# One PSUM bank moved from VectorE's ring to ScalarE's ring in a four-layer transformer kernel

## The reference

```python
x = x + attn_a(layernorm(x))      # rope attention: q, k, v and the output are rotated
x = x + ffn(layernorm(x))         # attention with biases, then a mixture of 8 experts, top 2
x = x + attn_b(layernorm(x))      # scores = cov(q, k) / d + q_var * k_var / d
x = x + ffn(layernorm(x))         # the same ffn weights again
# each attention: softmax(q k^T) v with 16 heads; ffn: gelu(t @ w1[e] + b1[e]) @ w2[e] + b2[e]
```

## Time and profile before

| | us |
|---|---|
| median of 3 runs | 1138.43 (1137.03 to 1139.28) |
| the profiled execution, its own time | 1136.1 |
| its span in the trace | 1134.2 |
| TensorE busy | 1029.3 (91%) |
| VectorE busy | 558.4 (49%) |
| ScalarE busy | 602.7 (53%) |
| GpSimd busy | 383.0 (34%) |

### The profile page before, as it was taken

How to read it: one execution, slowest core, us unless ns; L and a number is a source line. 1 busy time by engine, 2 the same in 40 slices (tenths; PEclk the granted TensorE clock), 3 DMA queues, 4 the chain that set the end, 5 groups by cost and what they waited for, 6 DMA issues and landing times. The chain is left out here.

```text
span 1134.2 us, 22104 instructions
## 1 busy us (share of the span) xinstructions
PE 1029.3 (91%) x8516; PEld 774.6 (68%) x8516; DVE 558.4 (49%) x1358; ACT 602.7 (53%) x1118; POOL 383.0 (34%) x823
## 2 busy tenths in 40 slices
PE   2798898889998799999995899999999789999998
PEld 2565565556654699989994656556665479998997
DVE  3638777657873411121113687878778341111111
ACT  1336565657786344344431667768877544434342
POOL 5546676547852100000003534555784210000000
PEclk9669788879999799999995799999999879999999
DMA  8000000000000000000000000000000000000000
GB/s 262 2 2 1 2 3 2 3 2 3 3 3 3 1 1 1 1 1 1 1 1 1 2 2 3 2 3 3 2 4 2 2 1 1 2 1 19 1 10 10
DMA packets 9958, 10.41 MB, mean 9 GB/s; under 512 B 1528, under 2 KB 7552, under 8 KB 9856
## 3 DMA queue, kind: packets, MB, share of 16 engines
q1 hardware_dynamic: 8848, 7.64, 2.1%
q10 hardware_dynamic: 1008, 1.38, 0.4%
HBM read 7.44 MB, written 1.05 MB: 7 GB/s over the span
## 5 line engine op out<-in xcount | busy, mean ns | idle before, releaser
L873 DVE TENSOR_REDUCE M<-bankR 128x2 f32<-128x512 f32 x512 | 326.7, 685 | 140.6 <-PE bankR L357 139.6
L670 ACT ACTIVATE Pr<-bankE 128x512 f32<-128x512 f32 x512 | 277.1, 595 | 125.5 <-PE bankE L344 121.7
L764 ACT ACTIVATE KQ<-bankE,b1c 128x512 f32<-128x512 f32 x256 | 173.4, 689 | 219.0 <-PE bankE L596 217.1
L605 PEld LDWEIGHTS bankR<-w,KQ 128*128 128x128 f32 x2048 | 237.3, 192 | 4.9
L605 PE MATMUL bankR<-w,KQ 128*128 128x128 f32 x2048 | 237.7, 275 | 0.0
L1015 DVE SCALAR_TENSOR_TENSOR X<-bankR,WE,X 128x128 f32<-128x128 f32 x256 | 72.1, 344 | 324.7 <-PE bankR L605 324.7
L357 PE MATMUL bankR<-KQ 32*128 32x256 f32 x1024 | 175.3, 346 | 8.3 <-DVE M L873 4.8
L371 PE MATMUL bankO<-Pr,Vx 128*32 128x256 f32 x2048 | 170.7, 408 | 0.6 <-ACT OT L664 0.3
L344 PEld LDWEIGHTS bankE<-KQ 32*128 32x128 f32 x1024 | 79.9, 190 | 98.3 <-issue 65.8
L344 PE MATMUL bankE<-KQ 32*128 32x256 f32 x1024 | 133.3, 337 | 0.8 <-DVE b1c L920 0.8
L357 PEld LDWEIGHTS bankR<-KQ 32*128 32x128 f32 x1024 | 112.9, 196 | 21.1 <-DVE M L873 14.9
(11 more groups left out here) (175 smaller groups left out, 1187.8 us busy)
## 6 DMA issues: line engine op xcount, KB each, us to landing
THL<-in_w SPq DMA_DIRECT2D x1, 2048.0 KB, 10.0
KQ<-MT SPq DMA_DIRECT2D x128, 4.0 KB
X<-in_x SPq DMA_DIRECT2D x8, 128.0 KB, 7.2
out_x<-X SPq DMA_DIRECT2D x4, 256.0 KB, 2.3
ropeA<-in_ropeA ACTq DMA_DIRECT2D x1, 384.0 KB, 5.5
ropeB<-in_ropeB ACTq DMA_DIRECT2D x1, 384.0 KB, 5.9
w_lo_rope<-in_w_qkv_rope ACTq DMA_DIRECT2D x1, 192.0 KB, 2.7
b_qkv_rope<-in_b_qkv_rope ACTq DMA_DIRECT2D x1, 192.0 KB, 4.1
```

Of the source, the lines that this page charges most:

```text
L605: k = mm(expert_bank(e)[:, t * D:t * D + D], G[:, e % 2, c, t * P:t * P + P], w2[:, e * FC + c, :], start=(c == 0), stop=(c == FC - 1))
L670: nc.scalar.activation(Pr[:, (h // HG) % 2, h % HG], act_bank("S", layer, b, h).rearrange("p (k q) -> p k q", k=TT), ACT.Exp, scale=EXP_SC ...
L764: nc.scalar.activation(G[:, e % 2, c, :], hidden_bank((at * FC + c) % 4), ACT.Gelu_apprx_tanh, bias=b1c[:, e * FC + c:e * FC + c + 1]).the ...
L873: v.tensor_reduce(M[:, b % 2, :, h], dve_bank("raw", layer, b, h).rearrange("p (t k) -> p t k", t=TT), AX.X, ALU.max, negate=True).then_in ...
```

## The change

Ring E gets five banks instead of four, ring R two instead of three. In the mixture, `wb` takes the fifth bank of `bankE` in place of the third of `bankR`. No instruction is added, removed or moved.

```diff
-        bankE = ctx.enter_context(nc.psum_tensor("bankE", [P, HG, TT, T], F32))
-        bankR = ctx.enter_context(nc.psum_tensor("bankR", [P, 3, 512], F32))
+        bankE = ctx.enter_context(nc.psum_tensor("bankE", [P, HG + 1, TT, T], F32))
+        bankR = ctx.enter_context(nc.psum_tensor("bankR", [P, 2, 512], F32))
...
-        ring_e, ring_r = Ring(HG), Ring(3)
+        ring_e, ring_r = Ring(HG + 1), Ring(2)
...
-                wb = [bankR[:, 2], bankO]
+                wb = [hidden_bank(HG), bankO]
```

More of the change, by code:

```diff
@@ L772, in mixture @@
                         act.wait_ge(b2mix, 4 * ph)
-                    wb = [bankR[:, 2], bankO[:]][q % 2]
+                    wb = [hidden_bank(HG), bankO[:]][q % 2]
                     copy(WT[:, 4 * q:4 * q + 4, :], wb[0:E, :].rearrange("e (t p) -> e t p", t=4)).then_inc(weT_copied, 1)
@@ L1023, in mixture @@
                     xq = X[:].rearrange("p b t d -> p (b t) d")[:, 4 * q:4 * q + 4, :]
-                    tt(xq, [bankR[:, 2], bankO[:]][q % 2].rearrange("p (t d) -> p t d", t=4), xq,
+                    tt(xq, [hidden_bank(HG), bankO[:]][q % 2].rearrange("p (t d) -> p t d", t=4), xq,
                        ALU.add).then_inc(b2_added, 1)
```

## The result

The changed kernel takes 1216.22 us, median of 4 runs (1212.35 to 1221.39), where the kernel before took 1137.99 in the same comparison (4 runs, 1137.03 to 1139.28). The ratio is 1.070, with an interval of 1.065 to 1.075. The forecast of 1222 us and its range held; several of its terms did not, and their errors partly cancelled, which is the more useful part of what follows. The profiled execution took 1219.18 us with a span of 1217.2, against 1136.1 and 1134.2 before: 83.0 us more span.

A forecast was written before the change was run, and what follows sets the result against it. TensorE was taken as nearly full, with VectorE close behind, so making TensorE wait costs at once. The profiled 1136.1 us plus 70 of bank waits and 14 of clock gave 1220, as median 1222 us, 7.4% slower; range 1190 to 1250.

The forecast's parts named there:

- waits for a bank: TensorE waiting for readers of ring R's two banks, summed over all steps: 70 us, given as 50 to 80.
- the clock: Falls of TensorE's clock in five cov steps and one in four of a dozen ffn steps: 14 us, bounds 0 and 54.
- Each place in an ffn step: Waits of ring R's takers, place by place from wo through round 5: 3.5 us more on a step of 16.7.
- the fifth bank: Ring E's added bank: costed at nothing, with bounds 0 and the listed 30.9 us.
- +1.6, five steps: 8: Rope steps: VectorE's second rope operation, which GpSimd waits for, comes 1.2 us later; +1.6 a step, 8 us in all.
- the 2.7 us that I read for one fall: K transposes to round 7 took 6.89 us at low clock in a rope step, 4.22 at full clock.
- 1.0 each: 3: Phase one's three ffn-projecting steps: zT's wait for GpSimd covers rounds 5 to 0; unrope's delay in rounds 2 to 4 stays.
- +1.9 a step: Cov steps: bank waits, part coming back where K waits for GpSimd's stacking; five steps, 10 us.
- Filling each phase's pipeline: Bank waits in the steps that fill each phase's pipeline: 3 us in all.
- The clock falls in nearly every step: Rival, chance 0.17: clock falls in nearly all steps cost 54 us; 1262 us, at the least 1240.
- Waits half as large: Rival, chance 0.14: VectorE catches up, so bank waits cost 35 to 50 us; 1173 to 1190, up to 1200.
- The other two: Rivals: ScalarE's ring E was the tight one, 1107 us (chance 0.03); ring R's third bank was unused, 1138 us (0.02).

The follow-up runs named there:

- fill: e4r2 with four idle matmuls into the unused eighth bank ahead of each bank take of outT, wo and gate; 1195.94 us, ratio 1.053.
- e4r2: The changed kernel with ring E back at four banks, ring R at two, the eighth bank idle outside the mixtures; 1220.89 us, ratio 1.074.
- own: The changed kernel with ring E at four banks, ring R at two, the eighth bank for outT, wo and gate alone; 1169.79 us, ratio 1.027.
- bfill: The kernel before with idle matmuls: three ahead of rope steps' first K transpose, twelve ahead of zT in five first-ffn-layer sequences; 1134.32 us, ratio 0.998.
- bboth: bnorm with three idle matmuls ahead of the rope layer's K transposes; 1124.56 us, ratio 0.988.
- aboth: fill with GpSimd's normalisation moved ahead of its stacking where a rope sequence is unroped; 1189.18 us, ratio 1.044.
- bnorm: The kernel before with GpSimd normalising the next input ahead of stacking in steps where a rope sequence is unroped; 1122.28 us, ratio 0.987.

## Why the prediction was right, and where it was not

Both parts came within their stated bounds: waits for a bank cost about 60 us as measured by fill (forecast 70, stated 50 to 80), the clock about 20 (forecast 14, 0 to 54). Where rows with the same clock are compared, they come to about 65 and 18.

**Each place in an ffn step held.** us from the round's start to the work behind it, from the pairs of rows above and, for round 1, its scores at 909.43 and the group behind them at 910.20; "more" is against before:

| place | before | after | more | forecast |
|---|---|---|---|---|
| wo behind round 7 | 0.45 | 1.46 | 1.01 | 1.01 |
| round 0 | 0.74 | 0.45 | -0.29 | -0.24 |
| round 1 | 0.63 | 0.77 | 0.14 | 0.12 |
| round 2 | 0.69 | 1.16 | 0.47 | 0.47 |
| round 3, outT | 0.79 | 1.46 | 0.67 | 0.67 |
| round 4 | 0.48 | 0.91 | 0.43 | 0.50 |
| round 5, gate | 0.51 | 1.45 | 0.94 | 0.95 |

The sum is 3.4, and the step grew by 3.2 (19.94 against 16.7), so some 0.1 came back elsewhere; the forecast was 3.5. The method, to ask of each taker which reader it now waits for and when that ends, gave the waits of this step to 0.07 us. The small differences are where VectorE could start a little sooner than I had it: the residual starts 0.72 us after wo and not 0.81.

**The two rings.** That the fifth bank is worth about nothing is shown by e4r2. That most of the loss goes when three groups have a bank of their own is shown by own (46 of 78 us). The mixtures kept their time: their matmuls in L605 are busy for 237.7 us and VectorE's additions in L1015 for 72.1 us in both pages, and L1015 stands idle for 324.1 us where it was 324.7.

**The terms of the sum.** us in the spans of the profiled executions. "After", "fill" and "bfill" say how much more than before. "Waits" is what the missing bank costs at the same clock, as nearly as the runs tell it: fill less bfill in the rope and mixed steps, since both have a clock of 1.00 there and before has not; e4r2 less before in the last steps, since it lacks the idle matmuls that are not free there; fill less before elsewhere. The forecast is that of bank waits alone, the sum of 70 split over these rows. Of the two last steps with raw scores in each phase, for which 13 was put, the first is the fourth step of the ffn row, and the second is counted with the last steps.

| stretch | before | after | fill | bfill | waits | forecast |
|---|---|---|---|---|---|---|
| rope, four steps | 85.9 | -1.5 | -3.6 | -4.7 | 1.1 | 6.4 |
| mixed, three steps | 61.7 | 0.0 | -4.1 | -7.5 | 3.4 | 3 |
| cov, four steps | 67.3 | +15.0 | +6.5 | +1.7 | 6.5 | 7.6 |
| cov/ffn, three steps | 46.5 | +11.5 | +7.7 | 0.0 | 7.7 | 8.4 |
| ffn, four steps in each phase | 133.7 | +32.3 | +25.0 | +1.4 | 25.0 | 27.5 |
| to the first wo, and from phase one's last wo to phase two's first | 397.0 | +14.1 | +10.5 | +1.2 | 10.5 | 6.5 |
| last three steps of phase one; in phase two all behind these ffn steps, mixture too | 303.2 | +7.2 | +10.9 | +0.3 | 4.5 | 6.5 |
| the steps between these | 38.9 | +4.4 | +6.1 | +3.2 | 6.1 | 4.1 |
| sum | 1134.2 | +83.0 | +58.9 | -4.3 | 65 | 70 |

**Rope, "+1.6, five steps: 8", was wrong.** The step that failed is that I let a rope step's waits for VectorE add to its length. What the runs showed: at full clock it is 20.3 us with three banks (bfill) and 20.6 with two (fill), +0.3. The loop through GpSimd takes up the rest; in fill zT still waits for GpSimd in each of the four steps, 1.2 us. And the clock went the other way than in the other steps: 0.84 before, 0.92 after. So the 2.7 us that I read for one fall are right as the duration of that stretch, but not as a price for a rope step, since the loop sets its length nearly as high (in before 20.1 us at full clock, 20.3 and 20.5 at 0.83; only the step at 0.73 took 24.9).

**The three mixed steps, "1.0 each: 3", were right, though the table shows 0.0.** Windows over them before, after and in fill:

```profile
203.50:265.20 61.70, 53.72 (x508) 32.91 (x504) 39.77 (x82) 38.02 (x79) 31.52 (x74) 0.83 0.01 2
215.40:277.10 61.70, 53.37 (x504) 31.45 (x504) 40.82 (x83) 38.43 (x79) 31.79 (x71) 0.92 0.01 2
208.90:266.40 57.50, 53.00 (x528) 33.09 (x528) 40.75 (x83) 38.26 (x79) 31.77 (x71) 1.00 0.01 2
```

The equal lengths are a coincidence of two things, since the clock was lower before than after. At a clock of 1.00 such a step takes 18.1 with three banks (bfill) and 19.2 with two (fill): 1.1 each. The cover that I had named, zT's wait for GpSimd's normalisation, took the rest: it shrank from 7.4 us in the three steps to 3.9.

**cov, "+1.9 a step",** cost 1.6 at full clock. With its falls it cost 15.0, so the clock took 8.5 us in four steps, 2.1 each where I had 1.75. In ffn steps the clock took 7.3 in eight and in cov/ffn 3.8 in three, where I had put 5 in all. Together that is 6 more than the clock term of 14. But in rope and mixed steps 6.0 came back, since they have less low clock after than before; I had named that possibility and put it at nothing. In cov the fall came behind the stretch that I had named, after rounds 2 and 3, at the wait ahead of outT.

**Filling each phase's pipeline, "3", was sized by guess,** and together with the first full step of each phase (3.5) it is 4 too low even where the clock was mostly held, and 8 as it stands. The first wo comes 7.4 us later in phase one (105.90 against 98.50), and 5.3 of it are left in fill (103.80). I hadn't followed one such step. In phase two the clock has a share: it is low while the pipeline fills, for 37.5 us before and for 54.6 after, and for 51 in fill too. These two windows, of before and after, show it:

```profile
599.83:637.37 37.54, 27.11 (x110) 22.10 (x110) 17.68 (x35) 10.52 (x18) 15.65 (x38) 0.50 0.00 1
628.40:683.00 54.60, 40.21 (x192) 29.15 (x192) 25.43 (x50) 16.81 (x30) 23.49 (x58) 0.50 0.00 1
```

So the middle of the range was met partly by luck, through errors of both signs. Among the waits, rope was put 5 us too high, ffn 2.5, cov and cov/ffn together 2 and the last steps 2; the filling 4 too low and the steps between 2 too low: together 5 too high. The clock, 18 net, was put 4 too low. What remains is one us, 84 forecast and 83 measured between the two profiled spans. Between the medians it is 78, which puts the forecast 6 too high: the profiled execution of the changed kernel took 3 us more than its median, that of the kernel before 2 less. The stated range was wider than these errors needed.

**The rivals.** "The clock falls in nearly every step" fell: 1216 and not 1240. By the windows the mean clock stayed at 0.85 to 0.94 in the second phase. The Trainium skill, in "TensorE: Matmul & The Clock Gate", section "A second HAM failure mode: psum-queue depth-cycling", has the clock going up and down in a kernel that cycles through PSUM banks with short idle times; this case's trace agrees that it happens (0.50 from 754.70 to 765.00), in part of the steps, and it made about 20 us of the 78. "Waits half as large" fell in the steady steps; in the rope steps alone they were smaller still (0.3 us of 1.6). The other two fell by e4r2 and by the table above.

**What stays open.** Which steps see a fall is not explained: a cov step at full clock (18.4 us) and one with a fall (20.9 to 22.0) hold the same instructions. The rope step at full clock with the loop open and three banks was never seen, since bboth didn't hold the clock there; with two banks, one such step of aboth took 20.0. That the low clock binds bnorm's rope steps is therefore not shown. How the 10 us of the filling divide into waits and the longer low clock was not followed, nor what fill's two steps between, still at clocks of 0.93 and 0.85, would take at full clock.

## What to carry to other kernels

Count a ring's depth in takers, not in banks: write down for each taker the reader that it waits for and when that reader ends after the taker two or three before; here that gave each wait of an ffn step to 0.07 us, and showed at once that odd takers between pairs (outT, wo, gate) pay most, so that one bank for them alone is worth more than one for the neighbouring ring. Before adding up such waits over all steps, ask in each kind of step which loop sets its length: the rope steps, with GpSimd in the loop, took the waits almost for nothing, and moving one GpSimd operation out of that loop (bnorm) brought 1.3%. Compare such steps only where their clock is the same: the mixed steps showed no loss, and had one of 1.1 us each. Where an engine must wait anyway and its clock is at stake, idle matmuls in the wait can pay, but only where the clock, and not another loop, is the limit (25 us of 1221 in fill, 0.2% in bfill, nothing in bboth).

## What the runs showed of the hardware that I had not expected

- A TensorE that is busy for most of a stretch on record can still lose its clock: 4.66 of 5.30 us busy, then 0.50 for 10.3 us. In fill, where four idle matmuls of 0.74 us in all stood ahead of outT, wo and gate, the four windows kept 1.00; two steps between them did not.
- The low clock can cost next to nothing. In the kernel before a rope step took 20.1 us at a clock of 1.00 and 20.5 at 0.83, with TensorE busy for 83% in the one and 95% in the other.
